# Gates of the first expert stage turned in fp32 and broadcast through DRAM instead of spread by TensorE

## The chip, the cores and the metric

The program runs on one core of one Trainium2 chip. The metric is the device time of one execution in microseconds (us); lower is better. The kernel before takes 517.11 us, the median of 3 runs (516.71 to 517.45).

## The reference, cut to what matters

A two-layer network works on 1024 tokens of 128 features. The change touches one part of it, the mixture of experts of layer 0: one shared expert and 7 routed ones, each a SwiGLU of width 512, in fp32.

```
logits = flat @ router_w.T                       # 1024 x 7
probs = softmax(logits);  top 2, divided by their sum -> combine (1024 x 7)
out = swiglu(flat, shared_gate, shared_up, shared_down)
for e in range(7):
    eo = silu(flat @ gate[e].T) * (flat @ up[e].T) @ down[e].T
    routed = routed + combine[:, e:e+1] * eo
```

The gate `combine[:, e]` is one number for each token and expert. The kernel multiplies it into the input of the `up` product, which is linear in it: `(g*x) @ up.T`.

## The kernel before, in words

Features lie on the 128 partitions and tokens on the free axis. The 1024 tokens are two halves of 512 (h = 0, 1; `HN` is 512), one PSUM bank each. An expert of the first stage is 8 steps: 2 halves by 4 blocks f of 128 hidden features. Eight experts (0 is the shared one) make 64 steps. Two experts are one body of 16 steps; body 0 is written out ("peeled", `i == 0`), bodies 1 and 2 are a hardware loop, body 3 is written out again (`last`).

An fp32 product is made of three fp32r products (high*high, low*high, high*low; `mm3`, lines 403 to 405). So a step is 9 matmuls of 512 columns on TensorE: 3 for the gate projection (`GATE0`), 3 for the value projection (`UP0`), 3 for the down projection of a step two earlier, which adds into bank 6 or 7. In a step, ScalarE applies silu (L1027) and rounds the hidden tile to its high part `ph` (L1051); VectorE multiplies silu and value (L1632) and makes the low part `pl` (L1652). TensorE's down projection waits for `pl`. VectorE's order in step q is: L1632 of step q+1, L1652 of step q, then the next input, where there is one.

The next input is what the change is about. For each half of experts 1 to 7 (14 times, once in four steps, in the step with f = 1), TensorE "spreads" the gates of that expert over all 128 partitions: a bf16 matmul (L494) of a column selector with `g3b`, which holds the gates of all experts as rows, in three bf16 parts stacked (24 rows). The result is in PSUM bank 0 (`GBC0`). VectorE multiplies it in place with the input YT (`scale_input`, L1618, in steps with q % 4 = 3); ScalarE rounds the product to `xch` (L1042); VectorE makes the low part `xcl` (`input_lo`, L1623, in steps with q % 4 = 0) from PSUM and `xch`.

Before the stage, the routing: VectorE makes the normalised gates `gp` (tokens on partitions), splits them into three bf16 parts (L1513 to L1517), TensorE turns them (8 bf16 transposes, L469, into banks 6 and 7), VectorE copies them to `g3b` (L1524, twice). Only then does `main` begin on TensorE. VectorE makes the first product of the stage (L1632 of step 0) between the split and the copies.

GpSimd (POOL) makes the low parts of the weights, `wl` (L1263): three instructions per expert, in the steps 2 to 4 of the expert before, each released by ScalarE's rounding (L960). After the last expert's it goes on without a wait to preparing the weights of a later stage (L1277 to L1294), among them two instructions over 2080 columns (L1283 and L1291). SyncE (SP) issues all DMAs in program order: the weights of expert e are loaded once those of expert e-1 are split.

Queues and semaphores alone order the work; nothing plans it at run time.

Of the kernel before, what the change touches and what calls it, by code (L numbers as in the profile page):

```python
# [67 lines left out]
def build(nc, d):  # L68
    with ExitStack() as ctx:
# [117 lines left out]
        act_out = [slot(1), slot(2)]  # L187
        moe_copy = lambda h: slot(5 + h)
# [40 lines left out]
        def parts_of(w):  # L229
# [24 lines left out]
        GATES_T = [[b.bitcast(BF16) for b in two] for two in (bank[6:8], bank[0:2])]  # L254
# [11 lines left out]
            "copied", "back", "x")} for k in range(2)]  # L266
        stored, m_gt, m_gtp, g_stored = sem("stored"), sem("m_gt"), sem("m_gtp"), sem("g_stored")
# [29 lines left out]
        def own_wait(eng):  # L297

            eng.nop(nofuse=True)
# [5 lines left out]
        def _(sp):  # L305
# [46 lines left out]
            with sp.Fori(1, NE0) as e:  # L352
                sp.wait_ge(m["wsplit"], WCH0 * e)
                sp.dma_start(wraw[:, 0:W0C], w[bass.ds(e, 1), :, :].rearrange("e p n -> p (e n)")).then_inc(m["wload"], 16)
# [31 lines left out]
        def _(pe):  # L386
# [77 lines left out]

            def turn_gates(rows, call):
                pe.wait_ge(m_parts, call + 1)
                for h in range(2):
                    for i in range(HT):
                        last = pe.transpose(blk(GATES_T[call][h], i)[0:rows, :],  # L469
                                            parts_of(rows // 3)[:, h * HT + i, :], identb[:, :])  # L470
                    last.then_inc(m_gT, 1)
# [13 lines left out]
            def moe0():  # L485
                m = moe[0]

                def spread(expert, un, g):

                    h = un % 2  # L490
                    if g is not None:
                        pe.wait_ge(m["xcp"], g)
                    own_wait(pe)
                    pe.matmul(GBC0, selb[:, bass.ds(expert, 1)].to_broadcast([P, P]),  # L494
                              g3b[:, h * HN:(h + 1) * HN], start=True, stop=True).then_inc(m["gbc"], 1)
# [70 lines left out]
                def main():  # L566
                    pe.wait_ge(m_g3, 2)
# [6 lines left out]
            def moe1():  # L574
# [41 lines left out]
                for h in range(2):  # L616
                    pe.wait_ge(m_g3, 3 + h)
                    spread(0, 2 * h)
# [81 lines left out]
            turn_gates(3 * NE0, 0)  # L700
# [225 lines left out]
        def _(act):  # L926
# [93 lines left out]
            def body0(i, last):  # L1020
# [10 lines left out]
                for q in range(len(STEPS0)):  # L1031
# [186 lines left out]
            for h in range(2):  # L1218
                act.wait_ge(m_g3, 3 + h)
                c = slice(h * HN, (h + 1) * HN)  # L1220
                act.activation(g3f[:, c], g3b[0:3 * NE1, c], ACT.Copy).then_inc(m_gf, 1)
# [140 lines left out]
        def _(dve):  # L1362
# [146 lines left out]
            def routing_parts(w, call, meanwhile=None):  # L1509
# [8 lines left out]
                if meanwhile is not None:  # L1518
                    meanwhile()
                for h in range(2):  # L1520
                    dve.wait_ge(m_gT, 2 * call + h + 1)
                    src = GATES_T[call][h][0:3 * w, 0:HN]
# [91 lines left out]
            step(dve.tensor_tensor(gp[:, :, 1:NE0], gp[:, :, 1:NE0], over_experts(gs1, NE0 - 1), ALU.mult))  # L1614

            def scale_input(un, g):
# [17 lines left out]
            def next_input(i, q, last):  # L1634
# [5 lines left out]
                if f == 0:  # L1640
                    if not (peeled and un == 2):
                        dve.wait_ge(m["xcp"], 4 * i + un - 2)
                    scale_input(un, 4 * i + un - 2)
# [13 lines left out]
            routing_parts(NE0, 0, lambda: gated(0, 0))  # L1657
# [340 lines left out]
```

## Time and profile before

| | |
|---|---|
| time, median of 3 runs | 517.11 us (516.71 to 517.45) |
| profiled execution, span first to last instruction | 516.3 us (its own time outside the span is not listed; the median is 0.8 us above the span) |
| chain of waits that ended last, by engine | TensorE 61%, VectorE 20%, ScalarE 9% |
| TensorE busy | 451.9 us, 88% |
| VectorE busy | 402.0 us, 78% |
| ScalarE busy | 311.3 us, 60% |
| GpSimd busy | 117.5 us, 23% |
| first expert stage | from about 84.8 to 222.9 us of the span |
| DMA | 29.86 MB, mean 58 GB/s |

How to read it: one execution, taken by the hardware profiler. PE is TensorE, PEld its weight loads, DVE is VectorE, ACT is ScalarE, POOL is GpSimd, SPq the DMA-issuing queue of SyncE. The recorded durations of back-to-back instructions overlap: a matmul of 512 columns shows 0.39 us but the next begins 0.23 us after it, a VectorE instruction shows 0.69 us and the next begins 0.60 us after it. So costs are read from start to start.

### The profile page before, as it was taken

To read this page: it belongs to the slowest core of one execution; us is meant where nothing else is said; L and a number is where in the kernel's file an instruction comes from. 1 tells how busy PE (TensorE), PEld (TensorE's weight loads), DVE (VectorE), ACT (ScalarE), POOL (GpSimd) and SP (SyncE) were. 2 spreads that over 40 slices of the span, in tenths; PEclk is the share of its full clock that TensorE was granted. 3 is DMA by queue.
4 is the path that set the end of the run, shared out by engine and by line. 5 is a ranking of instruction groups with operands and counts; after the bars stand their busy time and mean duration, and the time that the engine had idled before them with its cause. 6 is when DMAs were issued, how large, how long until landed. Compare 5 with 4: busy or idle time off the path is not lost.

```text
span 516.3 us, 8845 instructions
## 1 busy us (share of the span) xinstructions
PE 451.9 (88%) x2928; PEld 331.3 (64%) x2945; DVE 402.0 (78%) x1013; ACT 311.3 (60%) x586; POOL 117.5 (23%) x113
## 2 busy tenths in 40 slices
PE   4787588999999999978688878999967989999996
PEld 3343354777777787735354757888865557888884
DVE  4378968677777767576787897999986668999996
ACT  4237025567667766534324499989842347888884
POOL 2003001133112329300000245334600022222220
PEclk9868699999999999999899999999987979999999
DMA  8972000120111010000001000000001035445101
GB/s 274 400 233 62 3 2 1 61 62 14 49 61 61 20 41 1 1 1 1 1 2 42 1 3 1 1 1 2 2 1 43 0 94 197 149 158 171 53 1 41
DMA packets 11097, 29.86 MB, mean 58 GB/s; under 512 B 2529, under 2 KB 4753, under 8 KB 11057
## 3 DMA queue, kind: packets, MB, share of 16 engines
q1 hardware_dynamic: 11056, 29.35, 17.0%
q8 instruction: 22, 0.36, 0.3%
q14 instruction: 19, 0.15, 0.1%
HBM read 28.76 MB, written 0.59 MB: 57 GB/s over the span
## 4 chain that ended last, share of the span: by engine, by line
PE 61%; DVE 20%; ACT 9%; issue 5%; DMA 3%; SPq 1%; DVEq 0%; ACTq 0%
PE pair L403 13%; PE pair L404 13%; PE pair L405 13%; DMA arena<-in_zT 3%; PE pair L795 3%; PE pair L816 2%; PE pair L483 2%; PE pair L821 2%; PE turn L403 1%; PE turn L397 1%; DVE Y L1398 1%; DVE work L1599 1%; DVE st L1375 1%; ACT arena_r L1137 1%; PE turn L405 1%
## 5 line engine op out<-in xcount | busy, mean ns | idle before, releaser
L403 PE MATMUL pair<-yTh,wh 128*128 128x512 f32 x134 | 57.4, 428 | 3.3 <-ACT work L1027 3.2
L1263 POOL TENSOR_TENSOR wl<-wraw,wh 128x512 fp32r<-128x512 f32 x24 | 31.2, 1302 | 112.8 <-ACT wh L960 112.8
L404 PE MATMUL pair<-yTl,wh 128*128 128x512 f32 x134 | 53.5, 399 | 0.0
L405 PE MATMUL pair<-yTh,wl 128*128 128x512 f32 x134 | 53.3, 397 | 0.0
L1632 DVE TENSOR_TENSOR pair<-work,pair 128x512 f32<-128x512 f32 x48 | 33.3, 694 | 24.4 <-PE pair L405 20.5
L483 PE MATMUL pair<-g3b,zerob 128*128 128x512 bf16 x163 | 43.0, 402 | 8.7 <-POOL selb L1241 7.0
L1027 ACT ACTIVATE work<-pair 128x512 f32<-128x512 f32 x64 | 38.3, 598 | 14.5 <-PE pair L405 13.8
L1204 ACT ACTIVATE pair<-pair,vec 128x512 f32<-128x512 f32 x56 | 37.1, 662 | 12.0 <-PE pair L405 10.9
L1869 DVE TENSOR_TENSOR pair<-pair,arena 128x512 f32<-128x512 f32 x56 | 39.2, 699 | 5.8 <-ACT pair L1204 1.9
L1051 ACT ACTIVATE ph<-pair 128x512 fp32r<-128x512 f32 x48 | 28.7, 599 | 22.9 <-DVE pair L1632 22.9
L403 PE MATMUL pair<-ph,wh 128*128 128x512 f32 x96 | 39.0, 406 | 2.7 <-DVE pl L1652 2.6
L404 PE MATMUL pair<-pl,wh 128*128 128x512 f32 x96 | 38.1, 397 | 0.0
L405 PE MATMUL pair<-ph,wl 128*128 128x512 f32 x96 | 38.1, 397 | 0.0
L1256 POOL TENSOR_TENSOR yTl<-YT,yTh 128x512 fp32r<-128x512 f32 x4 | 5.1, 1276 | 136.7 <-ACT yTh L952 106.2
L938 ACT ACTIVATE YT<-turn 128x512 f32<-128x512 f32 x16 | 9.6, 597 | 40.1 <-PE turn L397 40.0
L483 PEld LDWEIGHTS pair<-g3b,zerob 128*128 128x128 bf16 x172 | 17.1, 104 | 25.7 <-issue 12.1
L1652 DVE TENSOR_TENSOR pl<-pair,ph 128x512 fp32r<-128x512 f32 x48 | 32.8, 683 | 0.6 <-ACT ph L1051 0.5
L403 PEld LDWEIGHTS pair<-yTh,wh 128*128 128x128 f32 x134 | 25.7, 192 | 10.7 <-ACT work L1027 3.5
L816 PE MATMUL pair<-arena 64*128 64x128 f32 x256 | 27.7, 292 | 5.1 <-DVE arena L1759 2.6
L1307 POOL TENSOR_TENSOR work<-work 128x512 f32<-128x512 f32 x16 | 22.0, 1375 | 37.4 <-ACT work L1106 37.4
L405 PEld LDWEIGHTS pair<-yTh,wl 128*128 128x128 f32 x134 | 25.4, 190 | 6.1
L404 PEld LDWEIGHTS pair<-yTl,wh 128*128 128x128 f32 x134 | 25.5, 190 | 5.3
(299 smaller groups left out, 1159.1 us busy)
## 6 DMA issues: line engine op xcount, KB each, us to landing
arena<-gates_by_expert SPq DMA_DIRECT2D x14, 512.0 KB, 6.1
wraw<-in_w SPq DMA_DIRECT2D x8, 768.0 KB, 4.3
arena<-in_zT SPq DMA_DIRECT2D x8, 514.0 KB, 9.6
wraw<-in_w SPq DMA_DIRECT2D x7, 512.0 KB, 3.3
arena<-in_z SPq DMA_DIRECT2D x6, 512.0 KB, 11.9
mat<-in_mat SPq DMA_DIRECT2D x1, 776.0 KB, 15.9
hel<-in_mat SPq DMA_DIRECT2D x48, 2.0 KB
row<-in_row SPq DMA_DIRECT2D x1, 576.0 KB, 16.1
```

Source lines behind the costliest of these rows:

```text
L403: pe.matmul(out, ah, bh, start=start, stop=False)
L404: pe.matmul(out, ah, bl, start=False, stop=False)
L405: return pe.matmul(out, al, bh, start=False, stop=stop)
L483: pe.matmul(bank[b], zerob[:, :], g3b[:, 0:HN], start=True, stop=True)
L816: pe.matmul(o, rot(4 * u + k)[rows, cols], rot(4 * u + 2 + k)[rows, cols], start=True, stop=False, skip_group_check=True)
L1027: act.activation(act_out[q % 2], GATE0, ACT.Silu).then_inc(m["act"], 1)
L1051: act.activation(ph[q % 2][:, :], UP0[q % 4], ACT.Copy).then_inc(m["hi"], 1)
L1204: act.activation(act_out[q % 2] if by_pe else UP1[q % 4], UP1[q % 4], ACT.Relu, bias=vec[:, bass.ds(at, 1)])\
L1263: pool.tensor_tensor(wl[k][:, cols], wraw[:, cols], wh[k][:, cols].bitcast(F32), ALU.subtract)\
L1632: dve.tensor_tensor(up, act_out[q % 2], up, ALU.mult).then_inc(m["mul"], 1)
L1652: dve.tensor_tensor(pl[q % 2][:, :], UP0[q % 4], ph[q % 2][:, :].bitcast(F32), ALU.subtract)\
L1869: dve.tensor_tensor(UP1[q % 4], hidden, gate, ALU.mult).then_inc(m["mul"], 1)
```

## The change

What it does:

- The gates are no longer split into bf16 parts. TensorE turns `gp` itself, in fp32 (8 transposes of 8 columns), and VectorE copies the two halves in fp32 to `gate0_t` (8 rows, in the work buffer).
- SP stores `gate0_t` to a scratch tensor in DRAM and loads each of the rows 2 to 7 from there, broadcast over 128 partitions, into work slots 14 to 17, two slots (the two halves) per expert, two pairs in turn. The loop over the weight loads is written out and the gate loads stand in it.
- For expert 1 alone TensorE still spreads the gates, with two fp32 matmuls (one per half) out of 8 rows, into the same PSUM bank.
- `scale_input` writes its product into the work slot; for experts 2 to 7 it also reads the gates there. `input_lo` and ScalarE's rounding read the product from the work slot, for all experts.
- TensorE's `main` waits for the two copies of `gate0_t`.

```diff
+        gate0_t = slot(3, 2)[0:NE0, :]
+        gate0_rows = lambda k, h: slot(14 + 2 * k + h)
...
+            def gates0(e):
+
+                if e >= 3:
+                    sp.wait_ge(g0_loaded, 16 * (e - 2))
+                    sp.wait_ge(m["xcp"], 2 * (e - 2))
+                sp.dma_start(work[:, (14 + 2 * (e % 2)) * HN:(16 + 2 * (e % 2)) * HN],
+                             gates0_dram[e:e + 1, :].to_broadcast([P, NT * P])).then_inc(g0_loaded, 16)
+
+            for e in range(1, NE0):
                 sp.wait_ge(m["wsplit"], WCH0 * e)
-                sp.dma_start(wraw[:, 0:W0C], w[bass.ds(e, 1), :, :].rearrange("e p n -> p (e n)")).then_inc(m["wload"], 16)
+                sp.dma_start(wraw[:, 0:W0C], w[e]).then_inc(m["wload"], 16)
+                if e == 1:
+                    sp.wait_ge(g0_copied, 2)
+                    sp.dma_start(gates0_dram[:, :], gate0_t).then_inc(g0_stored, 16)
+                    sp.wait_ge(g0_stored, 16)
+                    gates0(2)
+                if 3 <= e:
+                    gates0(e)
...
+            def turn_gates0():
+                pe.wait_ge(m_parts, 1)
+                for h in range(2):
+                    for i in range(HT):
+                        last = pe.transpose(blk(bank[6 + h], i)[0:NE0, :], gp[:, h * HT + i, 0:NE0], ident)
+                    last.then_inc(m_gT, 1)
...
-                def spread(expert, un, g):
-
-                    h = un % 2
-                    if g is not None:
-                        pe.wait_ge(m["xcp"], g)
-                    own_wait(pe)
-                    pe.matmul(GBC0, selb[:, bass.ds(expert, 1)].to_broadcast([P, P]),
-                              g3b[:, h * HN:(h + 1) * HN], start=True, stop=True).then_inc(m["gbc"], 1)
+                def spread(h):
+
+                    if h == 1:
+                        pe.wait_ge(m["xcp"], 1)
+                    a = CON_AT["sel0"][0] + 1
+                    pe.matmul(GBC0, con[0:NE0, a:a + 1].to_broadcast([NE0, P]), gate0_t[:, h * HN:(h + 1) * HN],
+                              start=True, stop=True).then_inc(m["gbc"], 1)
...
-                    if f == 1 and not (last and q > len(STEPS0) - NF0) and not (shared and h == 0):
-                        spread(2 * i + (un + 1) // 2, un + 1, None if shared else 4 * i + un - 1)
+                    if isinstance(i, int) and i == 0 and q in (NF0 + 1, 2 * NF0 + 1):
+                        spread(q // (2 * NF0))
...
-                        act.activation(xch[(un + 1) % 2][:, :], GBC0, ACT.Copy).then_inc(m["xch"], 1)
+                        act.activation(xch[(un + 1) % 2][:, :], gate0_rows((un + 1) // 2 % 2, (un + 1) % 2), ACT.Copy)\
+                            .then_inc(m["xch"], 1)
...
-                dve.wait_ge(m["gbc"], g + 1)
-                dve.tensor_tensor(GBC0, GBC0, yt(un % 2), ALU.mult).then_inc(m["xcm"], 1)
+                k, h = un // 2 % 2, un % 2
+                by_pe = isinstance(i, int) and i == 0 and un < 4
+                if by_pe:
+                    dve.wait_ge(m["gbc"], h + 1)
+                elif h == 0:
+                    dve.wait_ge(g0_loaded, 16 * (2 * i + un // 2 - 1))
+                dve.tensor_tensor(gate0_rows(k, h), GBC0 if by_pe else gate0_rows(k, h), yt(h), ALU.mult).then_inc(m["xcm"], 1)
...
-                dve.tensor_tensor(xcl[un % 2][:, :], GBC0, xch[un % 2][:, :].bitcast(F32), ALU.subtract)\
-                    .then_inc(m["xcp"], 1)
+                dve.tensor_tensor(xcl[un % 2][:, :], gate0_rows(un // 2 % 2, un % 2), xch[un % 2][:, :].bitcast(F32),
+                                  ALU.subtract).then_inc(m["xcp"], 1)
...
-            routing_parts(NE0, 0, lambda: gated(0, 0))
+            gated(0, 0)
+            for h in range(2):
+                dve.wait_ge(m_gT, h + 1)
+                dve.tensor_copy(gate0_t[:, h * HN:(h + 1) * HN], bank[6 + h][0:NE0, :]).then_inc(g0_copied, 1)
```

The order on VectorE at the stage's beginning, before (gs and gp are the gates' sums and the gates; pair and turn are PSUM banks, work is the work buffer in SBUF):

```order
L1614 TENSOR_TENSOR gp<-gp,gs 128x8x7
L1513 CAST gpart<-gp 128x8x8
L1514 TENSOR_TENSOR gr<-gp,gpart 128x8x8
L1515 CAST gpart<-gr 128x8x8
L1516 TENSOR_TENSOR gr<-gr,gpart 128x8x8
L1517 CAST gpart<-gr 128x8x8
L1632 TENSOR_TENSOR pair<-work,pair 128x512
L1524 COPY g3b<-pair 24x512 x2
L1632 TENSOR_TENSOR pair<-work,pair 128x512
L1652 TENSOR_TENSOR pl<-pair,ph 128x512
```

The same place on VectorE after:

```order
L1639 TENSOR_TENSOR gp<-gp,gs 128x8x7
L1662 TENSOR_TENSOR pair<-work,pair 128x512
L1688 COPY work<-pair 8x512 x2
L1662 TENSOR_TENSOR pair<-work,pair 128x512
L1680 TENSOR_TENSOR pl<-pair,ph 128x512
```

The five instructions of the split are gone; the copies now move 8 rows in fp32 and still stand between the first two products of the stage.

The last body's first input on VectorE, before (turn is the PSUM bank `GBC0` in L1618 and L1623):

```order
L1652 TENSOR_TENSOR pl<-turn,ph 128x512
L1618 TENSOR_TENSOR turn<-turn,YT 128x512
L1632 TENSOR_TENSOR pair<-work,pair 128x512
L1652 TENSOR_TENSOR pl<-pair,ph 128x512
L1623 TENSOR_TENSOR xcl<-turn,xch 128x512
L1632 TENSOR_TENSOR pair<-work,pair 128x512
```

And after:

```order
L1680 TENSOR_TENSOR pl<-turn,ph 128x512
L1648 TENSOR_TENSOR work<-work,YT 128x512
L1662 TENSOR_TENSOR pair<-work,pair 128x512
L1680 TENSOR_TENSOR pl<-pair,ph 128x512
L1653 TENSOR_TENSOR xcl<-work,xch 128x512
L1662 TENSOR_TENSOR pair<-work,pair 128x512
```

The order is the same; the two input instructions now have both inputs in SBUF (work, YT and xch are SBUF), where each had one in PSUM.

What GpSimd has in its queue from the last split of weights on, in the changed kernel (it is the same in both but for line numbers):

```order
L1290 TENSOR_TENSOR wl<-wraw,wh 128x512 x3
L1304 COPY hel<-hel 128x32x8 x2
L1307 ISA
L1307 TENSOR_SCALAR hc<-hc 128x8
L1310 TENSOR_SCALAR work<-hel,hc 128x2080
L1312 TENSOR_SCALAR hc<-hc 128x8
L1313 TENSOR_SCALAR hc<-hc 128x4
L1316 CAST work<-hel 128x512 x2
L1318 TENSOR_TENSOR hel_r<-hel,work 128x2080
L1321 TENSOR_TENSOR hel_r<-hel,work 128x512 x2
```

Nothing moved here; these are the instructions that run beside the last expert's steps (L1310 is L1283 of before, L1318 is L1291).

## Rows read from the trace of the kernel before

**Rows 1.** Busy time by stretch; columns: window, length, engines' busy, PEclk, DMA, GB/s

```profile
116.00:212.00 96.00, 96.00 (x412) 76.06 (x416) 71.11 (x112) 66.49 (x116) 34.79 (x26) 1.00 0.10 33
```

**Rows 2.** Timeline, TensorE, 199.9 to 204.8 (start, length, engine, line)

```profile
199.90 0.40 PE L403 MATMUL pair<-ph,wh 128*128 128x512 f32 x1
...
200.36 0.39 PE L405 MATMUL pair<-ph,wl 128*128 128x512 f32 x1
...
202.44 0.40 PE L405 MATMUL pair<-ph,wl 128*128 128x512 f32 x1
202.68 0.39 PE L494 MATMUL turn<-g3b,selb 128*128 128x512 bf16 x1
...
204.76 0.40 PE L405 MATMUL pair<-ph,wl 128*128 128x512 f32 x1
```

**Rows 3.** Instructions of L494: ns min/median/max, first and last start, forms

```profile
L494 PEld LDWEIGHTS turn<-g3b,selb x14: 95/96/97, 89.7 to 202.7; 128*128 x8, 128*128 128x128 bf16 x6
```

**Rows 4.** Timeline, VectorE beside the last expert

```profile
194.90 0.69 DVE L1618 TENSOR_TENSOR turn<-turn,YT 128x512 f32<-128x512 f32 x1
...
197.21 0.68 DVE L1623 TENSOR_TENSOR xcl<-turn,xch 128x512 fp32r<-128x512 f32 x1
...
198.69 0.68 DVE L1652 TENSOR_TENSOR pl<-pair,ph 128x512 fp32r<-128x512 f32 x1
...
205.78 0.68 DVE L1623 TENSOR_TENSOR xcl<-turn,xch 128x512 fp32r<-128x512 f32 x1
```

**Rows 5.** Timeline, where the stage begins, TensorE and VectorE

```profile
83.13 0.62 PE L469 MATMUL pair<-identb,gpart 128*24 128x128 bf16 x8
83.56 0.74 DVE L1524 COPY g3b<-pair 24x512 bf16<-24x512 bf16 x2
84.23 0.67 DVE L1632 TENSOR_TENSOR pair<-work,pair 128x512 f32<-128x512 f32 x1
84.83 0.67 DVE L1652 TENSOR_TENSOR pl<-pair,ph 128x512 fp32r<-128x512 f32 x1
...
85.61 0.44 PE L403 MATMUL pair<-ph,wh 128*128 128x512 f32 x1
```

**Rows 6.** Timeline, TensorE, fp32 matmuls of an earlier stage

```profile
43.14 1.02 PE L665 MATMUL pair<-YT,work 128*128 128x512 f32 x2
44.00 0.99 PE L666 MATMUL pair<-YT,work 128*128 128x496 f32 x2
```

**Rows 7.** Timeline, TensorE, four fp32 transposes

```profile
74.78 0.66 PE L397 MATMUL turn<-con,Y 128*128 128x128 f32 x4 [0.63 <-DVE Y L1398]
```

**Rows 8.** Groups of the first expert stage: count | busy us, mean ns | idle before

```profile
L960 ACT ACTIVATE wh<-wraw 128x512 fp32r<-128x512 f32 x21 | 13.1, 623 | 0.0
...
L1042 ACT ACTIVATE xch<-turn 128x512 fp32r<-128x512 f32 x14 | 8.3, 593 | 0.0
```

**Rows 9.** DMA issues by tensor: count, KB each, median us from issue to landing

```profile
arena<-gates_by_expert SPq DMA_DIRECT2D x14, 512.0 KB, 6.1
```

**Rows 10.** Timeline, a later stage: GpSimd beside VectorE with two SBUF inputs

```profile
328.62 0.69 DVE L1777 TENSOR_TENSOR work<-work,hstat 128x512 f32<-128x512 f32 x1
328.88 1.57 POOL L1307 TENSOR_TENSOR work<-work 128x512 f32<-128x512 f32 x1 [6.61 <-ACT work L1106]
...
371.76 3.01 POOL L1307 TENSOR_TENSOR work<-work 128x512 f32<-128x512 f32 x2 [4.66 <-ACT work L1106]
...
373.54 1.77 DVE L1802 TENSOR_TENSOR X<-X,row 128x512 f32<-128x512 f32 x1
```

**Rows 11.** Timeline, GpSimd beside the last expert

```profile
194.13 1.29 POOL L1263 TENSOR_TENSOR wl<-wraw,wh 128x512 fp32r<-128x512 f32 x1 [0.78 <-ACT wh L960]
195.37 0.73 POOL L1277 COPY hel<-hel 128x256 f32<-128x256 f32 x2
...
196.48 5.58 POOL L1283 TENSOR_SCALAR work<-hel,hc 128x2080 fp32r<-128x2080 f32 x1
...
203.72 4.68 POOL L1291 TENSOR_TENSOR hel_r<-hel,work 128x2080 fp32r<-128x2080 f32 x1
```

More of the change, by code:

```diff
@@ L253, in build @@
         LOGITS, MIXED_OUT = [bank[0], bank[6]], [bank[2], bank[6]]
-        GATES_T = [[b.bitcast(BF16) for b in two] for two in (bank[6:8], bank[0:2])]
+        GATES_T = [b.bitcast(BF16) for b in bank[0:2]]
         a_scores, a_masked, a_out, a_y2 = (sem("a_" + n) for n in ("scores", "masked", "out", "y2"))
@@ L266, in build @@
             "copied", "back", "x")} for k in range(2)]
+        g0_copied, g0_stored, g0_loaded = sem("g0_copied"), sem("g0_stored"), sem("g0_loaded")
+        gates0_dram = nc.dram_tensor("gates0_by_expert", (NE0, NT * P), F32, kind="Internal").ap()
         stored, m_gt, m_gtp, g_stored = sem("stored"), sem("m_gt"), sem("m_gtp"), sem("g_stored")
@@ L351, in _ @@
             m, w = moe[0], d["w0"]
-            with sp.Fori(1, NE0) as e:
-                sp.wait_ge(m["wsplit"], WCH0 * e)
-                sp.dma_start(wraw[:, 0:W0C], w[bass.ds(e, 1), :, :].rearrange("e p n -> p (e n)")).then_inc(m["wload"], 16)
+            def gates0(e):
[5 more added lines that the diff above has]
+            for e in range(1, NE0):
+                sp.wait_ge(m["wsplit"], WCH0 * e)
+                sp.dma_start(wraw[:, 0:W0C], w[e]).then_inc(m["wload"], 16)
[6 more added lines that the diff above has]
+                    gates0(e)
             def gates(e):
@@ L468, in turn_gates @@
                     for i in range(HT):
-                        last = pe.transpose(blk(GATES_T[call][h], i)[0:rows, :],
+                        last = pe.transpose(blk(GATES_T[h], i)[0:rows, :],
                                             parts_of(rows // 3)[:, h * HT + i, :], identb[:, :])
@@ L566, in main @@
                 def main():
-                    pe.wait_ge(m_g3, 2)
+                    pe.wait_ge(g0_copied, 2)
                     pe.wait_ge(y_lo2, 1)
@@ L616, in moe1 @@
                 for h in range(2):
-                    pe.wait_ge(m_g3, 3 + h)
+                    pe.wait_ge(m_g3, 1 + h)
                     spread(0, 2 * h)
@@ L699, in _ @@
             first_gates()
-            turn_gates(3 * NE0, 0)
+            turn_gates0()
             main()
@@ L1218, in _ @@
             for h in range(2):
-                act.wait_ge(m_g3, 3 + h)
+                act.wait_ge(m_g3, 1 + h)
                 c = slice(h * HN, (h + 1) * HN)
@@ L1507, in keep_top, with routing_parts @@
                 step(dve.tensor_reduce(gs1[:, :], pv, AX.X, ALU.add))
-            def routing_parts(w, call, meanwhile=None):
+            def routing_parts(w, call):
                 p3 = [parts_of(w)[:, :, a * w:(a + 1) * w] for a in range(3)]
@@ L1517, in routing_parts @@
                 dve.tensor_copy(p3[2], r).then_inc(m_parts, 1)
-                if meanwhile is not None:
-                    meanwhile()
                 for h in range(2):
                     dve.wait_ge(m_gT, 2 * call + h + 1)
-                    src = GATES_T[call][h][0:3 * w, 0:HN]
+                    src = GATES_T[h][0:3 * w, 0:HN]
                     c = slice(h * HN, (h + 1) * HN)
@@ L1613, in _, with scale_input @@
             step(dve.reciprocal(gs1[:, :], gs1[:, :]))
-            step(dve.tensor_tensor(gp[:, :, 1:NE0], gp[:, :, 1:NE0], over_experts(gs1, NE0 - 1), ALU.mult))
-            def scale_input(un, g):
-                dve.wait_ge(m["gbc"], g + 1)
-                dve.tensor_tensor(GBC0, GBC0, yt(un % 2), ALU.mult).then_inc(m["xcm"], 1)
+            dve.tensor_tensor(gp[:, :, 1:NE0], gp[:, :, 1:NE0], over_experts(gs1, NE0 - 1), ALU.mult).then_inc(m_parts, 1)
+            def scale_input(un, i):
+                k, h = un // 2 % 2, un % 2
[5 more added lines that the diff above has]
+                dve.tensor_tensor(gate0_rows(k, h), GBC0 if by_pe else gate0_rows(k, h), yt(h), ALU.mult).then_inc(m["xcm"], 1)
             def input_lo(un, g):
                 dve.wait_ge(m["xch"], g + 1)
-                dve.tensor_tensor(xcl[un % 2][:, :], GBC0, xch[un % 2][:, :].bitcast(F32), ALU.subtract)\
-                    .then_inc(m["xcp"], 1)
+                dve.tensor_tensor(xcl[un % 2][:, :], gate0_rows(un // 2 % 2, un % 2), xch[un % 2][:, :].bitcast(F32),
+                                  ALU.subtract).then_inc(m["xcp"], 1)
             def gated(i, q):
@@ L1640, in next_input @@
                 if f == 0:
-                    if not (peeled and un == 2):
-                        dve.wait_ge(m["xcp"], 4 * i + un - 2)
-                    scale_input(un, 4 * i + un - 2)
+                    scale_input(un, i)
                 else:
```

## The prediction, made before the changed kernel was run

> **What bounds the kernel now.** I first read the shares of the chain that ended last: most of it is TensorE's, a fifth VectorE's. Then the windows of the first expert stage: between 116 and 212 us TensorE is busy for 96.00 of 96.00 us at a granted clock of 1.00, the level of 2.4 GHz, while VectorE is busy for 71 and ScalarE for 66 [rows 1]. So in its steady part the stage lasts as long as TensorE's instructions, and every TensorE instruction removed there is time gained, as long as VectorE and ScalarE keep up. Then TensorE's timeline, from one last down matmul to the next: a plain step takes 202.44 - 200.36 = 2.08 us, one with a spread in it 204.76 - 202.44 = 2.32 us [rows 2]. The weight loads of L494 count the spreads: 14, from 89.7 to 202.7 us [rows 3].
>
> How close the others are: `pl` of the step whose down matmul begins at 199.90 is made from 198.69 to 199.37, so VectorE has 0.53 us in hand there [rows 2, 4]. A VectorE instruction of this size occupies 0.60 us (84.23 to 84.83) [rows 5]; a step with an input instruction has three, 1.80 of its 2.08 us.
>
> **The change, part by part.**
>
> *Spreads.* 14 bf16 spreads go: 14 x 0.24 = 3.36 us, by the mean over all fourteen steps (most are 2.31) rather 3.3. Two fp32 ones come. The row that is nearest is an fp32 matmul of 512 columns, in two passes: the next begins 44.00 - 43.14 = 0.86 us later [rows 6]. That it has 8 rows instead of 128 to add up should change nothing; the lower end is the bf16 spread's 0.24. I take 2 x 0.86 = 1.7. Net -1.6 us, at best -2.8.
>
> *The stage's beginning.* The five instructions of the split leave VectorE, and the first product of the stage moves ahead into their place. That gain can't be used: TensorE's fillers end just before 83.13 anyway, where the turning begins, and the turning is what the copies wait for [rows 5]. Four fp32 transposes take 0.66 us to the end of the last [rows 7], where the eight bf16 ones take 0.62 together. So the first copy can begin about 0.6 us after the turning does, at 83.7 (83.56 before). The copies: two bf16 ones take from 83.56 to 84.23, 0.34 each; in fp32 from PSUM the nearest row is any 512-column instruction of VectorE that reads PSUM, 0.60 each. I take 0.60: copies until 84.9, the second product at 84.9 instead of 84.23, and everything behind it on VectorE, `pl` and TensorE's first down matmul (85.61), as much later: +0.65 us. With 0.34 per copy it is +0.3. The Trainium skill ("VectorE: DVE Perf Modes", Mode 2×_2P) says that an fp32 copy gets two elements per cycle only where source and destination are both in SBUF, as PSUM has one read port; by that the copy runs at the slow rate, and the sum stays; by the bf16 row it would be 0.4 lower.
>
> *Input rounding.* ScalarE's rounding to `xch` reads SBUF instead of PSUM, 0.62 us (as L960) for 0.59 [rows 8]; three places of body 0 wait on it: +0.1.
>
> *DMA.* A 512 KB broadcast takes 6.1 us [rows 9]; the store of 32 KB is put at no more. Copied at 85, the gates of expert 2 land by 97; they are used in step 11, some 11 x 2.08 = 23 us after the stage begins, near 108. The later ones are issued behind the weights of the same expert in step 4 or 5 of expert e-2 and used in step 3 of expert e-1, seven steps or 14.6 us later. SP waits in these places for things that are already there. Cost 0; over 8 us of cover everywhere.
>
> So far: -3.3 + 1.7 + 0.65 + 0.1 = -0.85 us.
>
> *Where the inputs of VectorE lie.* `scale_input` (for experts 2 to 7) and `input_lo` (for all) now read two SBUF operands, beside GpSimd's instructions that read SBUF. The trace shows what that does. At 373.54 VectorE begins such an instruction while GpSimd's runs until 371.76 + 3.01 = 374.77; it lasts 1.77 instead of 0.69 us and ends 0.54 after GpSimd's: it has stood still for all of it. At 328.62 it is the other way round: VectorE is first, keeps its 0.69, and GpSimd's takes 1.57 [rows 10], against 1.29 of an instruction as large [rows 11]. Before the change the inputs are immune: L1618 at 194.90 and L1623 at 197.21 have their usual 0.69 and 0.68 us beside L1263 and L1283 [rows 4, 11]. The Trainium skill ("SBUF — State Buffer", Who interferes with whom) has the same as a rule: VectorE with two SBUF inputs and a GpSimd instruction that reads SBUF exclude each other for the whole instruction, whichever starts first. By this rule too the long ones below block for their full length, and its sum is my forecast.
>
> In the steady part this hides. Step 3 of each expert meets the last split of weights: `scale_input` would begin as at 194.90 and must wait until 194.13 + 1.29 = 195.42, so it ends 0.4 us later than now, of which 0.1 to 0.2 reaches the next product; 0.53 is in hand. Cost 0; without that cover at most 0.5 x 6 = 3 us.
>
> In the last body it doesn't. GpSimd has no weights left and goes straight on to L1283, 5.58 us, and L1291, 4.68 us [rows 11]. On the clock of before: `scale_input` waits until 195.42 and ends at 195.96. GpSimd's next instructions are put back by the same 0.54 us, L1283 from 196.48 to 197.02. VectorE goes on at its pace of 0.60: product 195.88, `pl` 196.48, `input_lo` 197.08. That is 0.06 us behind L1283. It stands until 197.02 + 5.57 = 202.6 and ends at 203.1; the next product and `pl` follow, `pl` ending at 204.3. TensorE's down matmul was due at 199.90 - 0.24 (one spread less) = 199.66: 4.7 us of standing. Then L1291, from about 204.8 to 209.5, meets `scale_input` of the second half, due 2.31 us ahead of L1623 at 205.78, so at 203.47 - 0.24 + 4.7 = 207.9: it ends at 209.5 + 0.54 = 210.05 instead of 208.5, 1.5 us late, and after the 0.53 in hand and the wait for the product that was there anyway some 0.7 is left: +0.7. Together +5.4 us. No row shows a GpSimd instruction over 2 us blocking anything, so the ends for these two are 0 and the full 5.58 + 4.68 less twice 0.53, 9.2 us; I take 5.4, since what is shown is full exclusion [rows 10].
>
> **Sum.** -0.85 + 5.4 = +4.5 us. Only the span of the profiled execution is listed, 516.3, and the median is 517.1; the terms are differences within the span, so they go onto the median: 521.6 us.
>
> **The rivals.** What this kernel's measurement can tell from no change is about 0.2%, 1.0 us.
>
> 1. *The first long one is missed.* `input_lo` gets in ahead of L1283: 0.06 us decide. Then L1283 runs from 197.6 to 203.2, the short ones follow and L1291 begins near 205.3, where `input_lo` of the second half is due (205.78 less 0.47 = 205.31). If L1291 is first, that one ends at 210.6 instead of 206.0, 4.1 us after what is in hand: 517.1 - 0.85 + 4.1 = 520.3 us. For it: the margin. Against: GpSimd's instructions follow one another without a gap.
> 2. *GpSimd keeps the port from one instruction to the next.* Then `scale_input` at 194.90 waits for the end of L1283 as well, 202.06, ends at 202.6, `pl` at 203.8, and TensorE's down matmul due at 197.6 stands for 6.2 us: 522.4, and 4 more if L1291 catches the next. Its instructions are back to back [rows 11]; that VectorE ends 0.54 us after one of them says nothing on this, as none followed [rows 10].
> 3. *Nothing shows: the other side.* Both long ones are missed, or instructions like L1283, with one tensor as input, don't exclude VectorE. Then -0.85 stands: 516.3 us, not slower, 0.16% faster; with copies at 0.34 us and cheap fp32 spreads 514.7 at the very best. For it: two margins that are as good as zero. Against: VectorE is due four times in the 17 us in which GpSimd is busy without a pause, and the two long ones take 10 of these.
> 4. *The gates come late from DRAM.* VectorE would stand in step 11 by (landing - 108). This decides only from a store and load of 24 us for expert 2, or a load of 14 us for a later one: left out.
>
> **How the numbers follow.** Forecast, the first long one blocks: 0.55, with a range of its own from 520.8 to 522.6 (the second meeting costs 0 to 1.5). Rival 1: 0.17. Rival 2: 0.10. Rival 3: 0.18. Slower by over 0.2% are the first three, 0.82. Rival 3 lies at 516.3, 0.2 from the bound of 516.1: 0.07 faster, 0.11 the same. The range must take in most of rival 3 and the near part of rival 2: 516.1 to 523.4.
>
> **What would show it.** In the profile after: 2 instead of 14 loads of the spread, 0.86 us each; plain steps of 2.08 us throughout the loop; two copies of 0.6 us and the first down matmul near 86.3; DMA broadcasts that nobody waits for. For the main step: L1653 (the new `input_lo`) near 197 us with a duration of about 6 us ending 0.5 us after L1310 of GpSimd, and a wait of TensorE for `pl` of about 4.7 us behind it; another `scale_input` of 2 us near 208. And in steps 3 of the other experts, `scale_input` of 1.0 to 1.2 instead of 0.69 us. I am wrong if `input_lo` has 0.69 us there with L1310 beside it (no exclusion), if it begins before L1310 (the margin), or if the step after a spread's place is longer than 2.08 us in the loop (the cover isn't there).

## The result, and the profile after

The changed kernel takes 521.73 us (median of four executions, 520.11 to 523.09) where the kernel before took 517.13 beside it: a ratio of 1.0105, 95% interval 1.0065 to 1.0145, so 4.6 us slower. Nine more executions on another occasion gave 523.44 (518.24 to 525.12) beside 516.91 for the kernel before (33 executions, 514.43 to 520.46): ratio 1.0104, 1.0065 to 1.0144. The ratios and intervals here are those on record for each comparison; they aren't quotients of the two medians (1.0089 for the first pair) and differ from them by up to 0.25%. The page below is of the execution of 520.11 us, its span 518.3.

First the stage by stretches (columns as in [rows 1]).

```profile
116.00:194.00 78.00, 77.68 (x337) 62.76 (x336) 60.34 (x94) 57.20 (x100) 18.02 (x14) 1.00 0.22 82
194.00:200.00 6.00, 6.00 (x27) 4.68 (x25) 5.98 (x6) 3.26 (x6) 5.47 (x5) 1.00 0.01 3
200.00:203.00 3.00, 0.33 (x2) 0.18 (x2) 2.77 (x3) 0.79 (x2) 3.00 (x2) 0.89 0.00 0
203.00:206.00 3.00, 3.00 (x8) 2.38 (x9) 1.29 (x2) 1.10 (x3) 3.00 (x5) 0.54 0.00 0
206.00:212.00 6.00, 5.71 (x25) 4.32 (x24) 5.37 (x7) 3.27 (x6) 6.00 (x3) 1.00 0.00 0
```

Up to 200 us TensorE is full, as before. From 200 to 203 it is busy for 0.33 us of 3.00, and in the next 3 us its granted clock is 0.54, close to the lower level (1.2 GHz), where [rows 1] had 1.00 throughout.

VectorE there, the counterpart of [rows 4]: L1648 is `scale_input`, L1653 `input_lo`.

```profile
195.23 1.07 DVE L1648 TENSOR_TENSOR work<-work,YT 128x512 f32<-128x512 f32 x1
197.42 4.15 DVE L1653 TENSOR_TENSOR xcl<-work,xch 128x512 fp32r<-128x512 f32 x1
207.83 1.89 DVE L1648 TENSOR_TENSOR work<-work,YT 128x512 f32<-128x512 f32 x1
210.84 0.68 DVE L1653 TENSOR_TENSOR xcl<-work,xch 128x512 fp32r<-128x512 f32 x1
```

GpSimd beside it (the counterpart of [rows 11]; L1310 was L1283, L1318 was L1291):

```profile
194.46 1.30 POOL L1290 TENSOR_TENSOR wl<-wraw,wh 128x512 fp32r<-128x512 f32 x1 [0.79 <-ACT wh L986]
197.27 5.57 POOL L1310 TENSOR_SCALAR work<-hel,hc 128x2080 fp32r<-128x2080 f32 x1
204.51 4.67 POOL L1318 TENSOR_TENSOR hel_r<-hel,work 128x2080 fp32r<-128x2080 f32 x1
209.13 3.54 POOL L1321 TENSOR_TENSOR hel_r<-hel,work 128x512 fp32r<-128x512 f32 x2
```

And TensorE: the last matmul ahead of the gap, three at the lower clock, and the second, small gap.

```profile
199.77 0.39 PE L425 MATMUL turn<-xch,wl 128*128 128x512 f32 x1
202.82 0.80 PE L423 MATMUL pair<-ph,wh 128*128 128x512 f32 x1 [2.67 <-DVE pl L1680]
203.41 0.63 PE L424 MATMUL pair<-pl,wh 128*128 128x512 f32 x1
203.84 0.63 PE L425 MATMUL pair<-ph,wl 128*128 128x512 f32 x1
...
210.97 0.50 PE L423 MATMUL pair<-ph,wh 128*128 128x512 f32 x1 [0.29 <-DVE pl L1680]
```

`input_lo` began 0.15 us after L1310 and lasted 4.15 us instead of 0.68; TensorE stood for `pl` and then ran its matmuls 0.43 us apart instead of 0.23 (0.59 after the first). From one last down matmul to the next (as in [rows 2]) the steps are 5.46, 2.98, 2.08 and 2.64 us: 3.38 + 0.90 + 0.56 = 4.84 us over the usual. Of the 3.38, the stand is 202.82 - 199.77 - 0.23 = 2.82 us; the other 0.56 and the 0.90 of the next step were lost at the lower clock, 1.46 us together. Behind all this the last down matmul of the same step begins at 221.33, where it began at 216.62 before: the stage ends 4.7 us later.

The spread of expert 1, and the stage's beginning:

```profile
89.97 0.40 PE L425 MATMUL pair<-ph,wl 128*128 128x512 f32 x1
90.30 1.12 PE L520 MATMUL turn<-work,con 8*128 8x512 f32 x2
91.35 0.50 PE L423 MATMUL pair<-yTh,wh 128*128 128x512 f32 x1
```

```profile
81.61 0.69 DVE L1662 TENSOR_TENSOR pair<-work,pair 128x512 f32<-128x512 f32 x1
83.58 1.28 DVE L1688 COPY work<-pair 8x512 f32<-8x512 f32 x2 [1.28 <-PE pair L489]
84.78 0.67 DVE L1662 TENSOR_TENSOR pair<-work,pair 128x512 f32<-128x512 f32 x1
85.38 0.67 DVE L1680 TENSOR_TENSOR pl<-pair,ph 128x512 fp32r<-128x512 f32 x1
```

The next matmul comes 1.05 us behind the spread's start and 1.38 behind the one ahead of it, which is 0.23 in a plain step (+1.15), and the one after that another 0.1 late: the two steps with a spread take 3.33 us, 1.25 more than 2.08. The copies are 0.60 us each and the second product starts 0.55 us later than in [rows 5]. The gates come in time (the group of [rows 9], and its new neighbour):

```profile
arena<-gates_by_expert SPq DMA_DIRECT2D x14, 512.0 KB, 6.2
work<-gates_by_expert SPq DMA_DIRECT2D x6, 512.0 KB, 5.1
```

Nobody waits for them: every step of the loop takes 2.08 us.

In this profile 2.9 us of the loss come back where the second expert stage begins. The rows of before and of after there show why (columns as in [rows 1]):

```profile
418.00:421.00 3.00, 3.00 (x9) 1.65 (x10) 2.49 (x4) 2.77 (x6) 2.59 (x3) 0.68 0.10 22
421.00:424.00 3.00, 3.00 (x8) 2.00 (x8) 1.98 (x4) 1.18 (x2) 0.00 (x0) 0.50 0.55 138
424.00:427.00 3.00, 3.00 (x10) 2.34 (x10) 1.29 (x2) 1.28 (x3) 0.00 (x0) 0.68 0.99 359
```

```profile
422.00:425.00 3.00, 2.62 (x13) 1.32 (x11) 2.28 (x5) 2.56 (x5) 3.00 (x4) 1.00 0.00 0
425.00:428.00 3.00, 3.00 (x14) 2.05 (x13) 2.77 (x5) 2.39 (x5) 0.52 (x1) 1.00 0.33 92
428.00:431.00 3.00, 3.00 (x15) 2.25 (x14) 2.58 (x4) 2.32 (x5) 0.00 (x0) 1.00 1.02 313
```

Before's execution had a low granted clock there (0.50 to 0.68), the other did not. This belongs to the execution, not to the kernel: the experiments below have it in either kind. So one pair of profiles is compared stage by stage, and the whole by medians. In every run that has both on record the time is 1.8 us above the span. The page of before, span 516.3, is then of an execution of about 518.1 us, above its median, which is why the two pages differ by 2.0 us only.

### The profile page after: what moved, and what is told of

Same layout as the page of the kernel before. It is cut to its first block, busy times and chain, and to the rows that moved or that the text cites. A ratio compares the mean times of both kernels' runs of the same rounds, so it can differ in the third digit from the quotient of the medians.

```text
span 518.3 us, 8791 instructions
## 1 busy us (share of the span) xinstructions
PE 451.0 (87%) x2935; PEld 330.4 (64%) x2935; DVE 408.5 (79%) x1008; ACT 311.7 (60%) x586; POOL 118.8 (23%) x113
## 4 chain that ended last, share of the span: by engine, by line
PE 61%; DVE 19%; ACT 9%; issue 5%; DMA 3%; SPq 2%; DVEq 0%; ACTq 0%
PE pair L423 13%; PE pair L424 12%; PE pair L425 12%; PE pair L821 3%; DMA arena<-in_zT 3%; PE pair L510 2%; PE pair L842 2%; PE pair L847 2%; PE turn L417 1%; PE turn L423 1%; DVE Y L1425 1%; DVE st L1402 1%; ACT arena_r L1164 1%; PE pair L464 1%; DVE pl L1680 1%
## 5 line engine op out<-in xcount | busy, mean ns | idle before, releaser
L423 PE MATMUL pair<-yTh,wh 128*128 128x512 f32 x134 | 54.5, 407 | 3.1 <-ACT work L1053 2.1
L510 PE MATMUL pair<-g3b,zerob 128*128 128x512 bf16 x172 | 46.5, 411 | 7.6 <-POOL selb L1268 6.8
L423 PE MATMUL pair<-ph,wh 128*128 128x512 f32 x96 | 39.2, 408 | 5.9 <-DVE pl L1680 5.8
L1283 POOL TENSOR_TENSOR yTl<-YT,yTh 128x512 fp32r<-128x512 f32 x4 | 5.1, 1272 | 139.6 <-ACT yTh L978 108.8
L423 PEld LDWEIGHTS pair<-yTh,wh 128*128 128x128 f32 x134 | 25.3, 189 | 12.6 <-ACT work L1053 3.5
```

Source lines behind the costliest of these rows:

```text
L423: pe.matmul(out, ah, bh, start=start, stop=False)
L510: pe.matmul(bank[b], zerob[:, :], g3b[:, 0:HN], start=True, stop=True)
```

## The experiments

Theory: VectorE's instructions with two SBUF inputs are held up by GpSimd's long ones in the last body. ("VectorE gets the port" below is short for the moment from which such an instruction runs: its recorded end less the 0.68 us that it takes unhindered.) Rival: something else of the change (gates from DRAM, slots, spreads) makes the end late. Each was timed against the kernel before; the median of that was 516.5 to 516.9 us throughout.

**e0, the changed kernel again.**

> The changed kernel once more, beside the others of this set and on their chip. Its four executions so far lay between 520.1 and 523.1 us, those of the kernel before within 0.7 us of one another. If the length of the block in the last body (VectorE's input_lo behind GpSimd's 5.57 us instruction) differs from execution to execution, this profile shows that one instruction at another length than 4.15 us, with TensorE's step there off by the same amount, and the time stays spread over some 3 us. If the spread comes from elsewhere (the second expert stage, or what lies outside the span), input_lo is again 4.1 to 4.2 us long and another stage differs.

523.44 us, nine executions. `input_lo` had the same length, 4.14; what differed was the second meeting, first VectorE, then GpSimd:

```profile
206.38 4.16 DVE L1648 TENSOR_TENSOR work<-work,YT 128x512 f32<-128x512 f32 x1
```

```profile
202.86 4.66 POOL L1318 TENSOR_TENSOR hel_r<-hel,work 128x2080 fp32r<-128x2080 f32 x1
207.48 2.52 POOL L1321 TENSOR_TENSOR hel_r<-hel,work 128x512 fp32r<-128x512 f32 x2
```

VectorE came to run only 0.68 us before 210.54, at 209.86, which is past L1318 and just at the end of the second L1321 (210.00). It had waited through three instructions, 3.5 us. In the first profile it got in at the end of L1318 (209.72 - 0.68 = 209.04), and the two L1321 took 3.54 us instead of 2.52. Steps of 5.34 and 3.19 us stand where the first profile had 2.64 and 2.08: 4.4 us lost instead of 0.56. So neither answer was right as put: the block varies, but it is the second, not the first.

**e1, GpSimd's later work put off.** One line ahead of it:

```
+            pool.wait_ge(moe[0]["xcp"], 2 * NE0 - 2)
             qk = mcol("WqD", 0, 8 * P).rearrange("p (s x) -> p s x", x=T)
```

> GpSimd starts its work behind the weights (some 18 us of it) only when the last input_lo is done. Port theory: nothing of two SBUF inputs is left beside a long GpSimd instruction, so the three late steps of the last body (together 4.8 us over the usual 2.08) are all 2.08 again, the granted clock stays 1.00 there, and the stage ends about where it did in the kernel before (+0.5 at its beginning, +2.5 of two spreads, -3.3 of fourteen): 516.9 us if the 2.9 us that the profiled run of the changed kernel got back in the second expert stage stay given back, up to 519.8 if not. Rival (gates from DRAM, slots or queues make the last body late, not GpSimd): the steps stay late, 521 to 522 us. The spread of the times over executions goes with the block if the block makes it.

516.58 us (12 executions, 514.65 to 519.31), ratio 0.9977, 0.9952 to 1.0002; 516.9 was expected. VectorE's four in the last body, and GpSimd's start:

```profile
193.75 1.07 DVE L1649 TENSOR_TENSOR work<-work,YT 128x512 f32<-128x512 f32 x1
195.94 0.68 DVE L1654 TENSOR_TENSOR xcl<-work,xch 128x512 fp32r<-128x512 f32 x1
202.07 0.68 DVE L1649 TENSOR_TENSOR work<-work,YT 128x512 f32<-128x512 f32 x1
204.15 0.68 DVE L1654 TENSOR_TENSOR xcl<-work,xch 128x512 fp32r<-128x512 f32 x1
```

```profile
204.90 0.74 POOL L1305 COPY hel<-hel 128x256 f32<-128x256 f32 x2 [10.63 <-DVE xcl L1654]
206.00 5.59 POOL L1311 TENSOR_SCALAR work<-hel,hc 128x2080 fp32r<-128x2080 f32 x1
```

Every step from there on takes 2.08 us. GpSimd's work makes the whole late end: 523.44 - 516.58 = 6.9 us in the medians, and what is left of the change is near zero. The times still spread by 4.7 us, as those of before do, so that part of the scatter isn't the block's. It goes with the mean granted clock of the execution: of the 33 executions of the kernel before on this occasion, the four at 0.952 took 518.1 to 520.5 us and the five at 0.967 took 514.4 to 515.8.

**e2, the product in PSUM.** The gates stay in DRAM and slots.

```
-  dve.tensor_tensor(gate0_rows(k, h), GBC0 if by_pe else gate0_rows(k, h), yt(h), ALU.mult)
+  dve.tensor_tensor(GBC0, GBC0 if by_pe else gate0_rows(k, h), yt(h), ALU.mult)
   (xch and xcl are made from GBC0)
```

> The gates still come from DRAM into the slots, but the product is written to the PSUM bank and read from there, so that input_lo has one SBUF input; scale_input keeps two. Port theory: input_lo is never blocked (0.68 us in its place under GpSimd's 5.57 us instruction). What is left is scale_input for the second half, which now comes about 203.5 us, between GpSimd's short instructions and ahead of its 4.67 us one: blocked by at most 1.2 us if it gets there first, by up to 4.2 us if that one starts first. So one late step instead of three, 517 to 521 us. Rival (reading the slots is slow by itself, whatever GpSimd does): scale_input, which still reads them, stays at 0.97 us mean even beside no GpSimd instruction.

516.64 us (10 executions, 513.78 to 518.55), ratio 0.9982, 0.9954 to 1.0010: below the 517 to 521 expected. VectorE:

```profile
196.93 0.68 DVE L1653 TENSOR_TENSOR xcl<-turn,xch 128x512 fp32r<-128x512 f32 x1
203.06 0.98 DVE L1648 TENSOR_TENSOR turn<-work,YT 128x512 f32<-128x512 f32 x1
```

With one SBUF input `input_lo` runs unhindered beside L1310 (196.78 to 202.35 here). `scale_input` waited 0.30 us, for a short instruction; no step is late. The rival of slow slots falls with e1, where that instruction has 0.68 us when GpSimd is idle. A form of operand, not the work, was the cost.

**e3, the kernel before with the product in SBUF.** The block without the change:

```
-  dve.tensor_tensor(GBC0, GBC0, yt(un % 2), ALU.mult)
+  dve.tensor_tensor(slot(14 + un % 2), GBC0, yt(un % 2), ALU.mult)
   (xch and xcl are made from that slot)
```

> The kernel before with one thing of the change: scale_input writes its product to a slot of SBUF instead of its PSUM bank, so that input_lo has two SBUF inputs (scale_input has one). Spreads, gates and queues are those of before. Port theory: all fourteen spreads still cost their 0.24 us, and the last body gains the block alone: input_lo of the last expert's first half is 3.5 to 5.6 us long behind GpSimd's 5.57 us instruction, TensorE stands 2.8 to 4.9 us, and the time is 3 to 6 us over that of the kernel before (520 to 523 us). Rival (the loss needs the DRAM gates or the fp32 spreads): within 0.5 us of the kernel before. It also tells whether the extra 1.0 us between span and time (1.8 us in the changed kernel, about 0.8 before) comes with the change's DRAM scratch and SyncE's longer program: then it is 0.8 here.

519.16 us (12 executions, 516.30 to 521.08), ratio 1.0032, 1.0008 to 1.0057: 2.3 us slower. VectorE, then GpSimd, in the profile:

```profile
197.44 3.57 DVE L1623 TENSOR_TENSOR xcl<-work,xch 128x512 fp32r<-128x512 f32 x1
207.22 0.69 DVE L1618 TENSOR_TENSOR work<-turn,YT 128x512 f32<-128x512 f32 x1 [0.37 <-PE turn L494]
209.81 1.84 DVE L1623 TENSOR_TENSOR xcl<-work,xch 128x512 fp32r<-128x512 f32 x1
```

```profile
196.70 5.58 POOL L1283 TENSOR_SCALAR work<-hel,hc 128x2080 fp32r<-128x2080 f32 x1
203.94 4.65 POOL L1291 TENSOR_TENSOR hel_r<-hel,work 128x2080 fp32r<-128x2080 f32 x1
208.54 2.56 POOL L1294 TENSOR_TENSOR hel_r<-hel,work 128x512 fp32r<-128x512 f32 x2
```

The block is there without gates from DRAM and without fp32 spreads, and L1618, with one SBUF input, passes beside L1291. The profiled execution (519.1 us of span) lost 4.3 us in the last body; the median loss of 2.3 us is under the 3 to 6 expected, so others must have lost less; how, isn't shown. The time outside the span is 1.8 us here too: it isn't the change's.

**e4 and e9, the 5.57 us instruction in four.**

```
+  n = (16 * P + T) // 4
+  for k in range(4):
+      c = slice(k * n, (k + 1) * n)
+      piece = pool.tensor_scalar(third[:, c].bitcast(F32R), raw[:, c], m_third, None, ALU.mult)
```

> The changed kernel, with GpSimd's 5.57 us instruction of 2080 columns cut into four of 520 columns (about 1.4 us each). In the profiled runs so far VectorE got the port 3.62 us after the start of that instruction (changed kernel 197.27 to 200.89 us, changed kernel again 195.62 to 199.24, kernel before with the product in SBUF 196.70 to 200.33), 1.95 us before its recorded end. Theory (the port is held by the instruction, up to a time that is set by that instruction): input_lo waits for one piece, so it is 1.2 to 2.1 us long instead of 4.15, TensorE's step there is at most 2.7 us instead of 5.46, and no clock is lost behind it. Rival (GpSimd keeps the port over a row of instructions without a pause): input_lo waits for several pieces, 3.6 us or more as before. The second meeting (scale_input of the second half beside the 4.67 us instruction) is as good as ahead of that instruction now, so it costs 0 to 1 us. Time: 4 to 7 us less than the changed kernel by the theory, the same by the rival.

> e4 once more. Its profile showed one piece of 1.58 us holding input_lo up for 0.4 us only and no late step, and 515.26 us, but its three other executions took 521.6 to 526.2 us. Theory (GpSimd sometimes keeps the port over several instructions in a row, as in the second profile of the changed kernel, where scale_input waited through three): the times fall into two groups, near 515 and over 521, and a profile of the second group shows input_lo 3 us long or more, past the end of the first piece. Rival (the long times are a matter of the clock alone): in this profile input_lo is 1.1 us long again and any loss lies in the granted clock elsewhere.

Medians 523.34 (4 executions, 515.26 to 526.18; ratio 1.0148, 1.0093 to 1.0202) and 523.56 (4, 521.82 to 524.59; 1.0120, 1.0064 to 1.0177), as the changed kernel, so the theory's 4 to 7 us less did not come. Of the eight executions one took 515.26 us and the others 521.6 to 526.2: two groups, as expected. The two profiles are the same up to 205.6 us, with `input_lo` of the first half 1.09 us long and no late step, and part there. The first (515.26 us), VectorE and GpSimd:

```profile
205.63 0.73 DVE L1657 TENSOR_TENSOR xcl<-work,xch 128x512 fp32r<-128x512 f32 x1
```

```profile
205.79 5.13 POOL L1322 TENSOR_TENSOR hel_r<-hel,work 128x2080 fp32r<-128x2080 f32 x1
```

And the second (524.02 us), with TensorE's stand:

```profile
205.60 7.72 DVE L1657 TENSOR_TENSOR xcl<-work,xch 128x512 fp32r<-128x512 f32 x1
```

```profile
205.70 4.63 POOL L1322 TENSOR_TENSOR hel_r<-hel,work 128x2080 fp32r<-128x2080 f32 x1
210.29 2.48 POOL L1325 TENSOR_TENSOR hel_r<-hel,work 128x512 fp32r<-128x512 f32 x2
```

```profile
214.57 0.79 PE L423 MATMUL pair<-ph,wh 128*128 128x512 f32 x1 [6.12 <-DVE pl L1684]
```

In one VectorE has the port first and GpSimd's instruction is 0.5 us longer; in the other GpSimd keeps it through three instructions, VectorE waits 7.0 us, and TensorE's steps are 8.92 and 3.84 us: 8.6 lost, 6.3 of it standing and 2.3 at the lower clock. Pieces cured the first meeting and brought the second half's `input_lo` next to GpSimd's 4.67 us instruction, where it costs most. "Ahead of the 4.67 us one, so 0 to 1 us" was wrong by that.

**e5, the wait behind the first long one** (the line of e1, ahead of the 4.67 us instruction).

> The changed kernel, with GpSimd waiting for the last input_lo only behind its first long instruction and the short ones, ahead of the 4.67 us one. The first meeting stays (input_lo 4.14 us long, TensorE's step 5.1 to 5.5 us and the next 3.0 to 3.5), the second one (0.56 us of TensorE in the first profile of the changed kernel, 3.27 + 1.11 us in the second, where VectorE's scale_input waited through the 4.67 us instruction and two of 1.28 us behind it) is gone. So the profile shows the steps behind at 2.08, and the time is that of the kernel with all of GpSimd's work put off (516.6 us) and 4.2 us, some 520.8; the difference to the changed kernel (523.4 us) is what the second meeting costs in the median. Rival (the second meeting seldom costs more than 0.6 us): as the changed kernel, 522.8 or more.

520.35 us (12 executions, 515.91 to 523.61), ratio 1.0054, 1.0020 to 1.0088; expected were 520.8. `input_lo` is 4.15 us long again, the steps 5.47 and 3.01, the rest 2.08. So in the medians the first meeting costs 520.35 - 516.58 = 3.8 us (4.3 in the profile) and the second 523.44 - 520.35 = 3.1. By the intervals of the ratios either is known to about 2.5 us only, so that the second is barely clear of nothing. And not every execution can have paid for the first in full: the lowest here, 515.91, is 1.3 us above the lowest of e1, 514.65. No profile shows such an execution.

**e6, the copies later,** with e1's wait. The copies go behind the third `pl`; the gates are turned into banks 0 and 7:

```
+  if isinstance(i, int) and i == 0 and q == 2:
+      for h in range(2):
+          dve.wait_ge(m_gT, h + 1)
+          dve.tensor_copy(gate0_t[:, h * HN:(h + 1) * HN], bank[7 * h][0:NE0, :]).then_inc(g0_copied, 1)
```

> With GpSimd's work put off as in e1, the two fp32 copies of the turned gates (0.60 us each) go behind the third product of the stage on VectorE, where it idled for 1.27 us, the gates are turned into two banks that are free till then, and TensorE waits for the copies only ahead of the first spread. Theory (VectorE's chain of copies, products and roundings sets the stage's beginning): the first down matmul comes 1.2 us earlier against the start of the gates' turning, nothing else changes, so 1.2 us less than with the wait alone: 515.4 us, a ratio of 0.997 to the kernel before. Rival (something else ends there, silu or TensorE itself): 0 to 0.5 us of it.

513.02 us (10 executions, 510.16 to 518.26), ratio 0.9915, 0.9887 to 0.9942: 3.9 us faster than before, and 3.6 less than e1 instead of 1.2. VectorE:

```profile
81.74 1.29 DVE L1664 TENSOR_TENSOR pair<-work,pair 128x512 f32<-128x512 f32 x2
83.10 0.69 DVE L1682 TENSOR_TENSOR pl<-pair,ph 128x512 fp32r<-128x512 f32 x1
...
87.11 0.67 DVE L1687 COPY work<-turn 8x512 f32<-8x512 f32 x1
```

The second product follows the first at once, where it came 3.17 us after it in the changed kernel (81.61, 84.78 above): not only the two copies are gone from between them, but also the stand of 1.28 us for TensorE's turning. Of the 3.6 us the profile shows 2.0: counted from TensorE's last L423 ahead of the gates' turning (81.85 here, 81.70 in the changed kernel), the last matmul of the first down projection begins 1.69 us earlier (85.13 and 86.67), the next step takes 0.70 instead of 1.20, and the step with the first spread 3.52 instead of 3.33. The rest isn't traced; the difference between the medians of e1 and e6, taken on two occasions, is itself known to about 2 us only.

**e7, the kernel before again.**

> The kernel before once more, one look. In its first profile TensorE's clock was granted at 0.50 to 0.68 in 418 to 427 us, where the second expert stage begins; in all five other profiles it was 1.00 in the same place and 2.9 us were got back there, in the kernel before with the product in SBUF as well. If that slow stretch belongs to the first profile's execution alone, this profile begins its second expert stage as those five did (three steps within 4.4 us instead of 6.3). If it belongs to the kernel before, it is there again.

The granted clock was 0.55 from 421 to 424 us and 0.88 in the 3 us behind: half of the slow stretch, 1.5 us of the 2.9 back. In e6, e8 and e10, kernels with the change, it was there in full. It goes with the execution.

**e8, bf16 spreads for the fp32 ones.** `GBC0 <- selb x g3b` in L520, with operands of the old spread's form; the gates of expert 1 are left out.

> e1 (GpSimd's work put off) with expert 1's two spreads as bf16 matmuls of zeros with one pass each, in place of fp32 ones; the gates of expert 1 are left out of the computation, the instructions and their places are the same. It is for the length of two steps alone: in e1 they take 3.33 us, 1.25 over the usual 2.08. If the whole of it is the fp32 matmul, they take 2.31 to 2.33 as the spreads of the kernel before did (0.24 over). If part of it lies elsewhere (the wait of the first spread's product on its way through a slot of SBUF), they stay over 2.4. Time: 2.0 us under e1.

```profile
90.69 0.39 PE L520 MATMUL turn<-g3b,selb 128*128 128x512 bf16 x1
```

The two steps are 2.34 and 2.32 us. The 1.25 are the fp32 matmul's own, 1.01 over bf16. (A single time, 517.5, tells nothing beside a scatter of 5 us.)

**e10, the second spread in a wait.** On e6: `spread(1)` goes from step 7 ahead of the down matmul of step 5, with a wait for the first product only.

> e6 (copies later, GpSimd's work put off) with the second fp32 spread moved from step 7 of the first expert pair to step 5, ahead of a down matmul for which TensorE waits 0.6 us anyway; its bank is free there, since the product goes to a slot. Theory (that wait is for VectorE's roundings, so that a matmul in it is hidden): step 7 falls from 3.33 to 2.08, step 5 grows from 2.70 by 0.65 to 3.35, so 0.6 us less than e6: 512.4 us. Rival (the spread keeps silu's or the down product's bank from being ready, so that it is not hidden): step 5 is 3.9 to 4.0 and the time that of e6, 513.0.

512.37 us (12 executions, 510.58 to 518.44), ratio 0.9923, 0.9892 to 0.9953. Step 5 takes 3.35, step 7 2.08, both as expected, so the profile has the 0.6 us. The times don't show it: the median is 0.65 lower than e6's, but the ratio is 0.0008 higher, and without the longest executions (over 518 us; two in e6, one here) both medians are 512.3. The two are the best versions found, some 4 us ahead of the kernel before.

## Why the prediction was right, step by step

Forecast 521.6, found 521.7 and 523.4 (the range ended at 523.4): the sign, the mechanism and the place are as forecast. That the first median is met to 0.1 us is luck: three sizes are off and one term is missing, and they partly cancel.

- *Spreads gone*, -3.3: as forecast; all steps of the loop 2.08.
- *Two fp32 spreads*, +1.7: measured +2.5. The row taken [rows 6] gives the pace among fp32 matmuls; between fp32r ones there is a gap on either side (0.33 ahead, 1.05 to the next). The upper end was missing: I bounded this term from below only.
- *The stage's beginning*, +0.65: measured +0.55 to +0.65, with 0.60 per copy. The Trainium skill ("VectorE: DVE Perf Modes", Mode 2×_2P) has PSUM sources at the slow rate, and the trace agrees: 0.60 per copy, against 0.34 for the bf16 ones. It was accepted as the price; e6 shows that it was avoidable and that more than it stood in that place.
- *Input rounding*, +0.1, and *DMA*, 0: the three steps of body 0 that wait are 2.71 instead of 2.68; no load is waited for. `scale_input` meets the splits as forecast (1.10 to 1.11 us in the loop, 1.07 at 195.23) and costs nothing.
- *First meeting*, +4.7: the wait is there, `input_lo` behind L1310 by 0.15 us (0.06 forecast). But VectorE got the port 3.6 us after L1310's start, not at its end: `input_lo` lasted 4.15 us, not about 6, and ended 1.3 before L1310 instead of 0.5 after it. So TensorE stood 2.8 us, not 4.7. The Trainium skill ("SBUF — State Buffer", Who interferes with whom) has exclusion for the whole instruction; the trace agrees for the others (the port changes hands 0.12 to 0.14 us before the recorded end) and not for this one, by 1.95 us. The clock then fell and cost 1.5, which no term had. Together 4.3 in this profile (4.5 in e0), 3.8 in the medians: near the forecast because a stand put too long by 1.9 us and a clock left out at 1.5 nearly cancel.
- *Second meeting*, +0.7: 0.56 in one profile, 4.4 in e0, 3.1 in the medians. What failed is "it ends at L1318's end". GpSimd may go on with its next instructions before VectorE gets in. That was rival 2, given 0.10 and put at the first meeting; it happens, in some executions, at the second.

Rival 1 (the first one missed) was not seen in any profile of the changed kernel. But the meeting that it had next, of the second half's `input_lo` with the 4.68 us instruction, is what e4 and e9 show: VectorE was first in one, and in the other it lost 8.6 us instead of the 4.1 reckoned, as GpSimd kept the port over its next two instructions as well. Rival 3 (nothing shows) is what e1 and e2 look like, 516.6, where it had 516.3.

Why VectorE got in at L1318's end in one execution and not in the other, and why L1310 gives up the port early, stays open.

## What to carry to other kernels

When an operand moves from PSUM to SBUF, list which GpSimd instructions run beside every VectorE instruction that now has two SBUF inputs, and let GpSimd's work that nobody needs yet wait (one line was worth 6.9 us here), or keep one input in PSUM. When an operation is forced onto another data type, look first whether its place is right: the copies cost 0.2 us three steps later. And price an operation by a row with the same neighbours, not only the same shape.

## What the runs showed of the hardware that was not expected

- GpSimd kept the shared port over three instructions in a row while VectorE waited, 3.5 us in e0 and 7.0 in e9; in other executions of the same programs VectorE got in between.
- GpSimd's TENSOR_SCALAR of 2080 columns (5.57 us) let VectorE in 3.62 us after its start in the changed kernel, e0, e3 and e5; one of 520 columns (1.60 us) 0.55 us after its start, in e4 and e9. Its TENSOR_TENSOR and CAST held it to 0.12 to 0.14 us before their ends wherever VectorE got in behind one of them.
- After TensorE stood 2.7 us it ran at a granted clock of 0.54 for 3 us, 1.5 us of loss over two steps; after the stand of e9, over 6 us, the two stretches of 3 us from 213 to 219 us were granted 0.50, 2.3 us of loss.
- An fp32 matmul of 8 rows and 512 columns between fp32r ones costs 1.25 us, a bf16 one 0.24.
